# Writing the float16 high part of a tile on VectorE with a multiply-and-max of the tile with itself instead of a cast

## What is computed

```python
x = x + L0(_gn(x), ...)    # _gn: a normalisation over groups of 2 channels and all positions
x = x + L1(_gn(x), ...)

def L0(z, mask, ...):
    zn = _ln(z, ln_in_w, ln_in_b)                        # normalised over the 64 channels
    a = m * sigmoid(zn @ w_ag + b_ag) * (zn @ w_ap + b_ap)
    b = m * sigmoid(zn @ w_bg + b_bg) * (zn @ w_bp + b_bp)
    p = einsum('bikc,bjkc->bijc', a, b)
    return (_ln(p, ...) @ w_z + b_z) * sigmoid(zn @ w_g + b_g)
```

## Time and profile before

| | |
|---|---|
| median of 3 runs | 1128.75 us (1128.51 to 1129.11) |
| the profiled execution | 1128.51 us |
| its span in the trace | 1126.4 us |
| mean granted clock of PE | 0.96 of full speed |
| busy: PE / PE weight load / DVE / ACT / POOL | 1023.0 / 796.5 / 787.8 / 638.6 / 414.2 us |
| share of the chain that ended last: PE / DVE / DMA | 79% / 9% / 4% |

### The profile page before, as it was taken

One profiled execution on the slowest core, in us unless ns is written; L12 is line 12 of the kernel. 1 busy time (PEld: TensorE's weight loads), 2 busy tenths in 40 slices (PEclk: granted clock), 3 DMA queues, 4 the chain that ended last, 5 costly groups with the idle time before them and its releaser, 6 DMA issues.

```text
span 1126.4 us, 35307 instructions
## 1 busy us (share of the span) xinstructions
PE 1023.0 (91%) x13948; PEld 796.5 (71%) x13948; DVE 787.8 (70%) x1238; ACT 638.6 (57%) x1006; POOL 414.2 (37%) x351
## 2 busy tenths in 40 slices
PE   6699798579999999978999995999999999879997
PEld 5543233268898888967999994788888888735554
DVE  6817988966876868678888888545435354467775
ACT  5757565455666656565767672544535444446665
POOL 0001554586190734706777771000000000056664
PEclk9989999879999999999999996999999999979999
DMA  9800000000302112089989910023040230599995
GB/s 346 308 9 1 0 1 0 1 2 12 142 4 113 41 58 96 19 218 264 212 190 204 203 44 1 4 55 100 4 131 23 66 87 3 147 215 278 288 268 150
DMA packets 184458, 121.29 MB, mean 108 GB/s; under 512 B 70788, under 2 KB 169476, under 8 KB 182280
## 3 DMA queue, kind: packets, MB, share of 16 engines
q1 hardware_dynamic: 184328, 119.34, 39.7%
HBM read 68.99 MB, written 50.33 MB: 106 GB/s over the span
## 4 chain that ended last, share of the span: by engine, by line
PE 79%; DVE 9%; DMA 4%; issue 3%; POOL 2%; ACT 2%; SPq 1%; DVEq 0%; POOLq 0%; ACTq 0%
PE PS L468 71%; DMA AB<-x 3%; PE PS L728 2%; PE PS L713 2%; PE PS L760 2%; DVE AB L1208 1%; POOL XT_ALL L956 1%; POOL AB L322 1%; DVE XT_ALL L1229 1%; PE PS L482 1%; DMA AB<-k_scratch 1%; DVE XT_ALL L1390 1%; SPq L336 0%; DVE WK L1265 0%; DVE REC L1382 0%
## 5 line engine op out<-in xcount | busy, mean ns | idle before, releaser
L468 PE MATMUL PS<-EFF,XT_ALL 64*128 64x64 f16 (+1 forms) x10368 | 343.7, 201 | 7.0 <-POOL XT_ALL L956 3.6
L468 PE MATMUL PS<-AB 128*128 128x256 f32 (+2 forms) x1226 | 320.3, 411 | 30.0 <-ACT AB L817 10.6
L468 PEld LDWEIGHTS PS<-EFF,XT_ALL 64*128 64x128 f16 (+1 forms) x10368 | 316.5, 97 | 41.0 <-issue 15.2
L468 PEld LDWEIGHTS PS<-AB 128*128 128x128 f32 (+2 forms) x1226 | 223.7, 185 | 123.5 <-ACT AB L817 28.7
L845 ACT ACTIVATE WK<-PS,T 128x512 f32<-128x512 f32 x256 | 175.4, 687 | 143.6 <-PE PS L468 132.0
L1017 POOL TENSOR_TENSOR WK<-XT_ALL 128x512 f32 (+1 forms) x64 | 83.9, 1312 | 351.2 <-DMA k_scratch<-WK 304.6
L322 POOL TENSOR_TENSOR AB<-WK,MS 128x512 f32 x96 | 130.7, 1390 | 105.6 <-DVE WK L1265 105.4
L1270 DVE TENSOR_TENSOR AB<-PS,WK 128x512 f32 x128 | 87.5, 690 | 65.0 <-ACT WK L845 64.4
L956 POOL TENSOR_TENSOR XT_ALL<-AB,XT_ALL 128x512 f32 (+1 forms) x59 | 69.8, 1191 | 165.7 <-DVE XT_ALL L1229 155.4
L1265 DVE TENSOR_TENSOR WK<-PS,WK 128x512 f32<-128x512 f32 x128 | 86.8, 688 | 31.3 <-ACT WK L845 24.2
L1287 DVE BATCH_NORM_STATS2 REC<-WK 128x512 f32 x64 | 44.4, 694 | 82.1 <-ACT WK L869 82.1
(11 more groups left out here) (190 smaller groups left out, 1407.7 us busy)
## 6 DMA issues: line engine op xcount, KB each, us to landing
AB<-x SPq DMA_DIRECT2D x64, 512.0 KB, 7.0
p_scratch<-WK SPq DMA_DIRECT2D x32, 512.0 KB, 2.6
k_scratch<-WK SPq DMA_DIRECT2D x128, 128.0 KB, 1.9
AB<-k_scratch SPq DMA_DIRECT2D x32, 512.0 KB, 7.6
out<-AB SPq DMA_DIRECT2D x16, 1024.0 KB, 6.1
AB<-p_scratch SPq DMA_DIRECT2D x29, 512.0 KB, 7.7
AB<-p_scratch SPq DMA_DIRECT2D x2, 640.0 KB, 6.3
RAW<-w SPq DMA_DIRECT2D x2, 256.0 KB, 2.6
```

Of the source, the lines that this page charges most:

```text
L468: return nc.tensor.matmul(dst, lhsT, rhs, start=start, stop=stop)
```

## The change

`high` no longer casts. It issues a three-operand instruction, (tile x 1.0) max tile, which is the tile itself, with the float16 part as output. Wait, semaphore and place in the order are unchanged, and so are the 48 uses.

```diff
@@ -1226,7 +1226,8 @@
             def high(n, slot):
 
                 dve.wait_ge(zn_done, n + 1)
-                V.tensor_copy(half(n, 0), zn[:, slot]).then_inc(hi_done, 1)
+                V.scalar_tensor_tensor(half(n, 0), zn[:, slot], 1.0, zn[:, slot], ALU.mult, ALU.max
+                                       ).then_inc(hi_done, 1)
```

## The result

| | before | after |
|---|---|---|
| median of 4 runs | 1128.93 us | 1141.98 us |
| range of the runs | 1128.51 to 1129.21 | 1141.75 to 1142.12 |
| profiled execution, span | 1128.51, 1126.4 us | 1142.07, 1140.3 us |
| DVE busy | 787.8 us | 822.8 us |

The ratio is 1.0115, with a 95% interval of 1.0103 to 1.0127. The change makes the kernel 13.1 us slower by the medians and 13.6 us by the profiled executions.

A forecast was written before the change was run, and what follows sets the result against it. DVE and POOL taking turns were taken to bound the tiles, their end setting PE's next round. Three rounds of 4.15 us give 12.5 us: 1128.51 + 12.5 = 1141.0 us, range 1136 to 1146.

The forecast's parts named there:

- The place: Rounds 0 to 2, from 98 to 236 us: DVE's tile end sets PE's next round; whole difference there, 12.5 us.
- The holding: High part beside POOL's low part: held until POOL ends, then needs 0.56 us in place of the cast's 0.28.
- The reading from L1313 and L322: Two-input DVE instructions elsewhere in the trace, ending 0.16 (128 elements) and 0.56 us behind POOL's end, gave the 0.56.
- The pace: Steady tiles of a round: loop 0.56 + 0.20 + 1.16 = 1.92 us per tile against 1.65, 0.27 more.
- The sum of a round: Each of rounds 0 to 2: tiles end 4.15 us later, and everything behind L1182 follows.
- The hand count of the first tiles: Start of a round, step by step: first extra 0.56 us not passed on, tile 5 0.96 us late.
- The clock: PE's granted clock: steady tiles hold 2.4 GHz, round-end gaps grow from 3 to 4 us; nothing added, 1.5 us either way.
- Rival 1: Tiles: only the cast is held, PE's 1.36 us a tile sets the pace, kernel takes 1120 us; chance 0.09.
- Its argument from L1343: Later stage with POOL busy: L1343 shows 0.75 us in all 64 cases, taken as support for an unheld three-operand instruction.
- Rivals 2 and 3: 2: PE's clock drops to 1.2 GHz inside tiles, about 1168 us (0.04 with others); 3: hidden elsewhere, 1129 us (0.03).

## Why the prediction was right

- **The place.** The whole difference is in the three stretches, 13.8 us of the profile's 13.9 in the span. Ahead of them the changed kernel's trace has 0.67 us more and behind them 0.6 less, in parts that nobody edited.
- **The holding.** Foreseen at 0.56 behind POOL's end, measured at 0.55; L1229 foreseen at 1.38 to 1.40, measured at a median of 1387 ns and a minimum of 678. The reading from L1313 and L322 carried over to another stage and another output type. The upper end, 0.75 for the instruction alone, was not needed; L1301's 0.69 was the right neighbour. One phrase of it does not hold to the letter: a held instruction does not do its "whole work" behind POOL's end. It ends there 0.13 to 0.14 us sooner than its length alone (0.28 against 0.42, 0.55 against 0.68). The forecast did not suffer, since it took the 0.56 from rows.
- **The pace.** 1.92 us per tile foreseen, 1.91 measured. Tile 4 was foreseen 0.70 us late and tile 5 0.96; counted from L1182 they are just that late (16.72 and 18.63 us in place of 16.02 and 17.67).
- **The sum of a round.** 4.15 us foreseen, 4.13 to 4.14 measured in each of the three rounds, when the way to the first product is left out. The hand count of the first tiles, where only a part of the loss is passed on, was needed: 16 times 0.27 would have given 4.3.
- **The clock.** This is the term that was mis-sized, at nothing with 1.5 us either way. Inside the tiles the granted clock stayed at 1.00, as argued. The changed kernel's clock in the stretches with the tiles of rounds 0 and 2:

```profile
98.00:136.00 38.00, 32.07 (x80) 12.02 (x80) 36.36 (x41) 21.09 (x32) 16.18 (x14) 1.00 0.00 0
```

```profile
190.00:222.00 32.00, 28.17 (x139) 11.77 (x137) 27.76 (x32) 17.16 (x27) 15.79 (x14) 1.00 0.00 1
```

Behind the gaps it cost 1.4 us more, 1.26 of it at one of the two, which is the step from the 12.4 us of the tiles to the 13.8 of the stretches. The gaps grew by 1.6 us (from 4.30 to 5.90 and from 2.98 to 4.57), not from 3 to 4 as foreseen. That this term stayed within the 1.5 us is in part luck, since equal gaps differed by as much from one trace to another.
- **The rivals.** Rival 1 was wrong as a mechanism, but three kernels ran its case, a high part of 0.68 us that is not held: it gave 1119.7 us for tiles at PE's pace, and 1116.1 was measured for the product made twice, 1118.3 and 1116.1 for the three-operand instruction beside a POOL that only writes. It missed that PE's gaps at the round ends shrink with DVE's earlier end: the gap ahead of round 2's tiles with the product made twice is 1.04 us and no slow pair follows it. Its argument from L1343 fell too: in the changed kernel's trace the same instruction is held, up to 1314 ns, when POOL comes first (last section). Rivals 2 and 3 did not occur.

## What to carry to other kernels

Before an instruction is put in another form, ask how many tiles it reads from SBUF and what POOL does beside it. An instruction that is held by POOL is shown long, and its length alone then says nothing of what another form would cost: subtract the neighbour's end first, as with 0.28 and 0.55 here. Where DVE and POOL take turns, a form with one input in SBUF and one in PSUM, though longer than a cast when alone (0.68 against 0.42), let the two run side by side and took 12.3 us from this kernel.

## What the runs showed of the hardware that was not expected

Who is held depends on who comes first, and that can flip far from the edit at no cost in time. In the last stage nothing was edited, yet L1344 takes 1155 ns on average, in place of the 751 of the earlier trace rows, 25.8 us more in all. Before, DVE came first, and POOL's instruction is shown with 1.31 us in place of 1.16:

```profile
1041.35 0.75 DVE L1343 SCALAR_TENSOR_TENSOR WK<-WK,T 128x512 f32<-128x512 f32 x1
...
1041.81 1.31 POOL L1017 TENSOR_TENSOR WK<-XT_ALL 128x512 f32 x1 [0.64 <-PE PS L713]
```

After, POOL comes first and DVE is held:

```profile
1052.70 1.16 POOL L1017 TENSOR_TENSOR WK<-XT_ALL 128x512 f32 x1 [0.72 <-PE PS L713]
...
1053.29 1.11 DVE L1344 SCALAR_TENSOR_TENSOR WK<-WK,T 128x512 f32<-128x512 f32 x1
```

Each tile of the stage takes 1.93 us on average in both, and from the first to the last of DVE's 64 it takes 121.7 us before and 121.4 after, so the stage's time is unchanged. A comparison by busy time alone would have looked in the wrong place: 25.8 us more are shown here and 14.7 in the edited lines. The flip does not belong to the edit either. In five of the ten traces this instruction shows 751 to 752 ns and in five 1155 to 1163; each group has kernels with the cast in some or all rounds and kernels with the three-operand form in all. From the fourth L1182 or its counterpart to the end all ten take 916.0 to 917.6 us. What decides who comes first there is open. And of two instructions that do the same work beside the same POOL instruction, the faster one can be the one that is held: 0.82 for the cast, 0.69 for the two-input form, beside a POOL that only writes.
